# A decoder layer on one core: the self softmax moves to ScalarE, the next batch's queries move behind the attention products, the cross mask goes to GpSimd

## The reference

```
x = x + self_attention(layernorm(x))       # 16 heads of 128; q, k rotated and RMS-normed
    scores = einsum(q, k) * scale; masked causally (-1e30)
    probs  = softmax(concat([scores, sink]))[..., :t]
    y      = probs @ v, then two projections
x = x + cross_attention(layernorm(x), ctx)  # 16 heads of 32
    scores = einsum(q, k) / sqrt(32); masked causally; attn = softmax(scores); out = attn @ v @ Wout.T
x = x + moe(layernorm(x))                   # rmsnorm, router, top 4 of 32 experts, shared expert
```

## Time and profile before

| what | value |
|---|---|
| median of 3 runs | 1218.83 us (1205.28 to 1225.98) |
| the profiled execution | 1214.66 us, span of its instructions 1212.9 us |
| busy over the span | PE 95%, DVE 67%, ACT 49%, POOL 28% |
| one pass of the loop, from PE's L518 to the next | 41.40 us |
| PE's granted clock, mean over the span | 0.979 |

### The profile page before, as it was taken

One profiled execution on the slowest core, in us unless ns is written; L12 is line 12 of the kernel. 1 busy time (PEld: TensorE's weight loads), 2 busy tenths in 40 slices (PEclk: granted clock), 3 DMA queues, 4 the chain that ended last, 5 costly groups with the idle time before them and its releaser, 6 DMA issues. The chain is left out here.

```text
span 1212.9 us, 20949 instructions
## 1 busy us (share of the span) xinstructions
PE 1153.7 (95%) x7761; PEld 910.5 (75%) x7762; DVE 811.2 (67%) x1392; ACT 595.5 (49%) x1404; POOL 336.4 (28%) x279
## 2 busy tenths in 40 slices
PE   6989999999999999999999988899979999999994
PEld 3446777677777767776777666788769999999993
DVE  1144777897888789878977876642256666666661
ACT  1134544654564456445644644321236666666661
POOL 0011013112211212221122112222215666566633
PEclk9998999999999999999999989999989999999997
DMA  7820000000000000000000005032279999999964
GB/s 261 245 96 1 3 3 16 14 9 9 14 15 3 15 14 9 9 16 14 9 9 16 14 10 200 8 122 65 85 250 261 288 285 275 285 291 286 277 143 53
DMA packets 62587, 121.10 MB, mean 100 GB/s; under 512 B 10118, under 2 KB 13750, under 8 KB 62378
## 3 DMA queue, kind: packets, MB, share of 16 engines
q1 hardware_dynamic: 44810, 82.46, 20.3%
q0 software_dynamic: 17728, 37.97, 14.5%
HBM read 93.55 MB, written 28.13 MB: 100 GB/s over the span
## 5 line engine op out<-in xcount | busy, mean ns | idle before, releaser
L1462 POOL TENSOR_TENSOR rall<-qkv_var,phalf 100x17 f32<-100x17 f32 x16 | 49.2, 3073 | 420.5 <-DVE qkv_var L1147 420.5
L379 PE MATMUL QS<-xh,wh 128*128 128x256 f32 x512 | 148.1, 289 | 0.0
L380 PE MATMUL QS<-xl,wh 128*128 128x256 f32 x512 | 145.5, 284 | 0.0
L381 PE MATMUL QS<-xh,wl 128*128 128x256 f32 x512 | 145.4, 284 | 0.0
L1539 POOL DMA_INDIRECT out_rows<-work,idx x64 | 103.0, 1610 | 122.1 <-ACT work L1027 85.1
L379 PE MATMUL W<-wch,oth 128*100 128x512 f32 x256 | 105.1, 411 | 0.0
L380 PE MATMUL W<-wcl,oth 128*100 128x512 f32 x256 | 100.6, 393 | 0.0
L381 PE MATMUL W<-wch,otl 128*100 128x512 f32 x256 | 100.4, 392 | 0.0
L380 PEld LDWEIGHTS QS<-xl,wh 128*128 128x128 f32 x512 | 99.0, 193 | 1.2
L379 PEld LDWEIGHTS QS<-xh,wh 128*128 128x128 f32 x512 | 98.8, 193 | 1.2
L381 PEld LDWEIGHTS QS<-xh,wl 128*128 128x128 f32 x512 | 98.8, 193 | 0.0
(11 more groups left out here) (214 smaller groups left out, 2870.9 us busy)
## 6 DMA issues: line engine op xcount, KB each, us to landing
raw<-in_w SPq DMA_DIRECT2D x24, 1024.0 KB, 8.3
raw<-in_w SPq DMA_DIRECT2D x24, 512.0 KB, 10.2
work<-in_w SPq DMA_DIRECT2D x8, 1024.0 KB, 8.1
work<-in_w SPq DMA_DIRECT2D x8, 512.0 KB, 9.5
hx_rows<-h3x SPq DMA_DIRECT2D x16, 212.5 KB
h_columns<-h3s SPq DMA_DIRECT2D x16, 200.0 KB, 1.9
h3T<-h_columns SPq DMA_DIRECT2D x4, 800.0 KB, 9.8
out_rows<-ytiles POOLq DMA_DIRECT2D x16, 200.0 KB, 2.5
```

The costliest lines, as they stand in the source:

```text
L379: mm(dst, ah, bh, start=start, stop=False)
L380: mm(dst, ah, bl, start=False, stop=False)
L381: return mm(dst, al, bh, start=False, stop=stop)
L1462: return nc.gpsimd.tensor_tensor(out=dst, in0=src, in1=phalf[:, 0:src.shape[1]], op=ALU.pow)
```

## The change

1. Self softmax. DVE takes the maximum of the raw scores straight from each PSUM bank (four reductions), and two 16-wide steps make of it the negative shift per head, with the sink. ACT then takes 16 exponentials, one for each head, from PSUM into SBUF, with the norm as `scale`, the shift as `bias` and the sum over the row as a second output. DVE's scaling, subtraction and sum of the whole go; its last product is cut into four quarters, each with its own signal.
2. ACT's order. The copies of the cross keys, cross values and the next columns stand between the groups of exponentials; the copy of the cross queries behind them; the copy of the cross scores behind the four copies of transposed probabilities.
3. PE's order. The next batch's columns stand in the middle of the cross queries, then keys and values, compressed queries, and the cross scores; the next batch's queries stand behind the attention products. The cross scores wait for all exponentials, since these read the same banks.
4. The cross mask. The four mask products L462 go; GpSimd masks the cross scores in SBUF (`affine_select`, 100 x 1600) after ACT's copy, and DVE's `cross_shifted` waits for it and now stands behind the four L1290.

```
 # tensor, cross_queries(b, more, follow)
                 for i in range(4):
+                    if i == 2 and follow:
+                        ln1_columns(b + 1)
                     for k in range(KC):
                         last = mm(wb[1][:, T * i:T * (i + 1)], w_q[...], h2T[...], ...)
 # tensor, cross_products
-                pe.wait_ge(s.s_scaled, 4 * scored)
+                pe.wait_ge(s.p_exp, scored)
-                for j in range(4):
-                    mm(qb[j][0:T, 0:QW], identb[:, :], mask4[:, :], start=True, stop=False)
 # tensor, step
+                if do.Q:
+                    if do.X:
+                        pe.wait_ge(s.ck, b)
+                    keys_values(b + 1)
+                    if do.X:
+                        pe.wait_ge(s.qp, b)
+                    compress(b + 1)
                 if do.X:
                     cross_products(b, b + 1, do.C)
-                if do.Q:
-                    compress(b + 1)
-                    pe.wait_ge(s.s_scaled, 4 * b + 4)
-                    if do.X:
-                        pe.wait_ge(s.sx, b)
-                    queries(b + 1)
                 if do.A:
-                    pe.wait_ge(s.p_norm, b + 1)
                     for i in range(4):
+                        if i == 1 and do.Q:
+                            pe.wait_ge(s.hqT, b + 2)
                         ...
+                        pe.wait_ge(s.p_norm, 4 * b + i + 1)
 ...
+                if do.Q:
+                    pe.wait_ge(s.p_exp, b + 1)
+                    if do.X:
+                        pe.wait_ge(s.sx, 2 * b - 1)
+                    queries(b + 1)
 # scalar
+            def exponentials(i):
+                for h in range(QH * i, QH * (i + 1)):
+                    last = fn(Pm[0:T, T * h:T * (h + 1)], qb[i][0:T, T * (h % QH):T * (h % QH + 1)], ACT.Exp,
+                              bias=mx[:, h:h + 1], scale=rall[:, h:h + 1], accum_out=den[:, h:h + 1])
+                return last
 # vector, step
-                        tt(Pm[0:T, QW * i:QW * (i + 1)]..., qb[i][0:T, 0:QW]..., per_head(rall[...], QH), ALU.mult)
-                    red(mx[:, :], P3, AX.X, ALU.max).then_inc(s.s_max, 1)
-                    tt(mx[:, :], mx[:, :], sink[:, :], ALU.max).then_inc(s.s_max, 1)
+                        red(mx[:, QH * i:QH * (i + 1)], qb[i][0:T, 0:QW]..., AX.X, ALU.max)
+                    nc.vector.scalar_tensor_tensor(out=mx[:, :], in0=mx[:, :], scalar=-1.0, in1=rall[:, 0:NH], ...)
+                    nc.vector.scalar_tensor_tensor(out=mx[:, :], in0=sink[:, :], scalar=-1.0, in1=mx[:, :], ...)
-                    tt(P3, P3, per_head(mx[:, :], NH), ALU.subtract).then_inc(s.s_shift, 1)
-                    red(den[:, :], P3, AX.X, ALU.add).then_inc(s.p_sum, 1)
-                    tt(P3, P3, per_head(rinv[:, :], NH), ALU.mult).then_inc(s.p_norm, 1)
-                if do.X:
-                    cross_shifted(b)
+                    for i in range(4):
+                        tt(P3[:, QH * i:QH * (i + 1), :], ..., ALU.mult).then_inc(s.p_norm, 1)
                 ... rotate_keys, four differences otl (L1290)
+                if do.X:
+                    cross_shifted(b)
 # gpsimd
+            def cross_masked(b):
+                wait_alone(pool, s.sx, 2 * b - 1)
+                nc.gpsimd.affine_select(out=PX..., in_=PX..., pattern=[[0, NX], [-1, T]],
+                                        compare_op=ALU.is_ge, fill=NEG, base=0, channel_multiplier=1).then_inc(s.sx, 1)
```

More of the change, by code:

```diff
@@ L406, in ln1_columns, with keys_values @@
                 to_columns(wb[0], h1).then_inc(s.h1T_ps, 1)
+            def keys_values(c):
+                pe.wait_ge(s.h1T, c + 1)
+                for k in range(KC):
+                    last = mm(wb[2][0:T, 0:2 * D], h1T[:, T * k:T * (k + 1)], w_kv[:, 256 * k:256 * (k + 1)],
+                              start=k == 0, stop=k == KC - 1)
+                last.then_inc(s.kv_ps, 1)
             def compress(c):
@@ L414, in compress @@
                 last.then_inc(s.hq_ps, 1)
[L415 to L418, removed]
             def queries(c):
@@ L432, in project, with cross_queries @@
                 return last
-            def cross_queries(b, more):
+            def cross_queries(b, more, follow):
                 pe.wait_ge(s.ln2_h, b)
@@ L468, in cross_products @@
                         last = mm(qb[j][0:T, T * i:T * (i + 1)], qpT[r, T * i:T * (i + 1)],
-                                  ckT[r, T * i:T * (i + 1)], start=False, stop=i == 3)
+                                  ckT[r, T * i:T * (i + 1)], start=i == 0, stop=True,
+                                  skip_group_check=True)
                 last.then_inc(s.sx_ps, 1)
@@ L623, in _ @@
             ln1_columns(0)
+            keys_values(0)
             compress(0)
@@ L812, in compressed @@
                 copy(kvs[:, :], wb[2][0:T, 0:2 * D]).then_inc(s.kv, 1)
+                act.wait_ge(s.hq_ps, c + 1)
+                act.wait_ge(s.q_ps, 4 * c)
+                copy(hqT[:, :], wb[1][:, 0:T]).then_inc(s.hqT, 1)
             def queries_out(c):
@@ L860, in step @@
                     copy(h2T[:, :], wb[0][:, 0:QW]).then_inc(s.h2T, 1)
+                if do.A:
+                    act.wait_ge(s.s_shift, 2 * b + 2)
+                    act.wait_ge(s.pT_ps, 4 * b)
+                    act.wait_ge(s.p_den, 2 * b)
+                    exponentials(0)
+                if do.X:
                     act.wait_ge(s.ck_ps, b)
@@ L863, in step @@
                     copy(ckT[:, :], wb[2][:, 0:QW]).then_inc(s.ck, 1)
+                if do.A:
+                    exponentials(1)
+                if do.X:
                     act.wait_ge(s.cv_ps, b)
@@ L866, in step @@
                     copy(cv[:, :], wb[3][0:T, :]).then_inc(s.cv, 1)
+                if do.A:
+                    exponentials(2)
+                if do.Q:
+                    ln1_columns(b + 1)
+                if do.A:
+                    exponentials(3).then_inc(s.p_exp, 1)
+                    act.wait_ge(s.s_sink, b + 1)
+                    fn(esink[:, :], sdiff[:, :], ACT.Exp).then_inc(s.e_sink, 1)
+                if do.X:
                     act.wait_ge(s.qp_ps, b)
@@ L869, in step @@
                 if do.Q:
-                    ln1_columns(b + 1)
+                    compressed(b + 1)
+                    key_square(b + 1)
                 if do.A:
[L872 to L875, removed]
-                    fn(esink[:, :], sdiff[:, :], ACT.Exp).then_inc(s.e_sink, 1)
+                    act.wait_ge(s.s_ps, 4 * b + 4)
+                    for i in range(4):
+                        act.wait_ge(s.pT_ps, 4 * b + i + 1)
+                        copy(T16[0:T, QW * i:QW * (i + 1)], wb[i][0:T, 0:QW]).then_inc(s.pT, 1)
                 if do.X:
@@ L1281, in step @@
                     dve.wait_ge(s.p_den, 2 * b + 2)
-                    tt(P3, P3, per_head(rinv[:, :], NH), ALU.mult).then_inc(s.p_norm, 1)
-                if do.X:
-                    cross_shifted(b)
+                    for i in range(4):
+                        tt(P3[:, QH * i:QH * (i + 1), :], P3[:, QH * i:QH * (i + 1), :],
+                           per_head(rinv[:, QH * i:QH * (i + 1)], QH), ALU.mult).then_inc(s.p_norm, 1)
                 if do.Q:
@@ L1479, in step @@
                     ln1(b + 1)
+                if do.X:
+                    cross_masked(b)
+                if do.Q:
                     qk(b + 1)
```

60 lines of the change are left out of this document (28 added, 32 removed).

## The result

The changed kernel takes 1248.13 us in the median, the kernel before 1224.19 us in the same comparison: ratio 1.0235, 95% interval 1.0187 to 1.0283. One of its six runs was disturbed (4443 us) and is left out of the ratio; the other five lie between 1239.47 and 1254.35. So the changed kernel is slower; whether by more than 2% is not settled, since 2% lies inside the interval. The forecast was 1242.5 us, by a mechanism in three pieces.

What follows compares the result with a forecast made beforehand. PE was taken to bound the loop; stalls of 2.4 us less 0.77 saved cost 1.6 a pass, 14 x 1.6 + 1 = 23.5 us: 1238 for the profiled execution, 1242.5 on the median, range 1218 to 1268.

Steps and rivals of the forecast that it cites:

- a mechanism in three pieces: PE stalls each pass: 0.85 us at the columns, 1.15 before keys and values, 0.4 before compress.
- Bound and cost of a stall: In the loop PE has no slack: waits are paid in full; its work falls 0.77 to 40.6 us a pass.
- First stall: At the next batch's columns, mid cross queries, PE waits 0.85 us for DVE, itself held by POOL's late power.
- The exponentials: ACT's 16 exponentials cost 0.41 us each (bounds 0.23 and 0.50), so h1T is done late, at 463.35.
- the sum of stalls: PE's waits in one loop pass: 0.85 + 1.15 + 0.4 = 2.4 us, before the 0.77 saved.
- The mask: GpSimd's mask before DVE's cross shift takes 2.5 us, hidden; up to 3.5 before PE stalls.
- The room behind: Later in the pass nothing stalls: 0.45 us of room before the queries, 0.6 before PE's transposes at 485.8.
- The ends: Outside the 14 loop passes: batch 0 about +2 us, batch 15 some 1.5 sooner, tail +1.5 less 0.8; together +1.
- (a): Rival, chance 0.17: operands hidden, 0.23 to 0.27 us an exponential; only the columns' stall stays, 1221 us.
- (b): Rival, chance 0.15: GpSimd's mask becomes the bound beyond 3.5 us; at 5 us, 1.5 more a pass, 1265 us.
- (c): Rival, chance 0.10: new stalls lower PE's clock for 3.3 us a pass, half of that lost, 1266 us.
- (d): Rival, chance 0.05: faster, 1205 to 1207 us, with columns ready 0.85 us sooner and exponentials under 0.32 us.

Runs made afterwards that it cites:

- x2: Changed kernel with the next batch's columns back behind the cross queries instead of in their middle; 1267.92 us, run once.
- x3: Changed kernel with the 16 exponentials without both per-partition operands (fixed scale 0.01, no bias; probabilities not the reference's); 1227.33 us, run once.
- x5: Changed kernel with one per-partition operand (the bias) and a fixed scale of 0.01 in the exponentials; probabilities not the reference's; 1246.63 us, run once.
- x1: Kernel before with only the mask change: mask products gone, GpSimd masks between ACT's copy and DVE's shift; 1241.30 us, ratio 1.0119.
- x9: Kernel before without mask products; GpSimd writes zeros after ACT's cross exponential, cross values' product behind the cross queries; ratio 1.0018.
- x12: x9 with ACT's copy cv and the sink's exponential moved behind the copies hqT and kvs; ratio to the kernel before 1.0033.
- x6: Changed kernel with GpSimd's mask done three times over, one after the other; 1325.10 us, run once.
- x10: Kernel before without mask products; GpSimd masks ahead of DVE's maximum, cross values' product behind the cross queries; ratio 1.0197.
- x4: Changed kernel with the edits of x2 and x3 together; probabilities not the reference's; 1217.27 us, run once.
- x8: Changed kernel with the next batch's queries ahead of the transposes again, the cross scores' copy ahead of the transposes' copies; 1337.78 us, run once.

## Why the prediction was right, and where not

**Bound and cost of a stall: right.** PE bounded before and bounds after, at a clock of 1.00, and its waits are paid in full: 0.85 + 1.12 + 0.35 less 0.77 is 1.55 of the 1.66 us; the remaining 0.1 is the hand-over between compress and the cross products. PE's busy time, forecast as 40.6, reads 41.14, since around each wait a modelled end runs on.

**First stall: right,** 0.85 us, with POOL's power behind its four list transfers. But passes 2 and 3 of x2 show that it is no term by itself: with the columns back, PE waits for h1T by as much longer. What sets the pass is ACT's chain.

**The exponentials: right.** Forecast 0.41 us by adding the operands of the earlier trace rows to a Square of the earlier trace rows, measured 0.41; x3 and x5 show both terms, 0.23 and 2 x 0.09. Set back by the 11.86 us, ACT's h1T starts at 462.78, forecast 462.85, and the sum of stalls is 2.32 against 2.4.

**The mask: right that it is hidden, its price too high.** Taken 2.5 us, measured 1.64; the nearest row, DVE's pass of 1.81, was the better estimate than the middle of the bounds. Because it was hidden, nothing followed.

**The room behind: right.** L496 was forecast 485.8, and is 485.83 in those positions. The queries did not wait.

**The ends: the mis-sized term.** Forecast +1 beside 14 passes of 1.6. Batch 15 is 1.7 us shorter (forecast 1.5), but the tail pass is 2.3 longer and what follows it 2.2, where 0.7 was forecast. The rows, which answer:

```profile
735.23 1.67 PE L472 MATMUL QS<-ckT,qpT 32*100 32x100 f32 x32 [3.73 <-ACT qpT L806]
...
779.31 0.45 PE L379 MATMUL QS<-h3h,w_suh 128*128 128x400 f32 x1 [3.32 <-DVE w_sul L1366]
```

In batch 15 the wait has moved from the transposes to the cross products, where qpT now stands behind 16 exponentials; it is in one piece, and the products behind it run at the slower level (1.67 us against 0.96). In the tail PE waits 3.32 us for DVE's w_sul, 1.54 before. DVE had waited on its way there:

```profile
773.38 1.82 DVE L1206 TENSOR_REDUCE mxx<-work 100x16 f32<-100x1600 f32 x1 [1.52 <-POOL work L1510]
```

POOL's mask stands there behind four list transfers and takes 2.11 us, and unlike in the loop nothing lies between DVE and it. This wait was priced rightly (1.5). What the prediction put at nothing is the clock behind the waits. The 8.28 us of PE's work that follow the wait for w_sul have a mean granted clock of 0.79, and took 6.71 us at 1.00 before; the stretch behind them gives back 1.0. A little later, behind the last cross output, stands a wait of 3.00 us for DVE's h3x, which the kernel before has too (3.01), and only in the changed one is the work behind it slow:

```profile
809.99:816.33 6.34, 6.34 (x29) 6.32 (x30) 3.30 (x4) 2.72 (x4) 0.00 (x0) 0.73 0.10 35
```

Before, this stretch took 4.81 us at 1.00. Whether the change brings this is open: x1, x3, x5, x9 and x12 show 0.96 over the 47 us behind the last cross output too, as the changed kernel does, and only one execution of the kernel before was traced.

Start and loop went the other way: batch 0 and 14 passes were forecast at 24.4 us and brought 21.8. Batch 0 is 1.8 us longer, as forecast (38.44 against 36.63, between the starts of the transposes L541, L546 after). But it starts 0.9 us sooner, for which no run gives a cause, and pass 1 is 0.3 us shorter and not 1.6 longer (42.83 against 43.13): in the kernel before it ran in part at the slower level (L541 took 2.87 us, 1.72 in the later passes), and that is a matter of the one execution. Two errors of 2.6 and 3.6 us, of opposite sign; that the profiled time came so near the forecast is luck in this part.

**The whole.** 1238 us was forecast for the profiled execution, 1239.5 came. (The sum is rounded up twice: 14 x 1.6 + 1 is 23.4, and 1218.83 + 23.5 is 1242.3. Neither matters.) The median was forecast 1.9% above the one before, and is 2.35% [1.87, 2.83] above: the profiled execution is the fastest of the five. What the others have more is in no trace here; the part behind the loop, which varies by 20 us between the traces, is one place where it can lie.

**The rivals.** (a) fell: the operands are not hidden. Its condition, an exponential under about 0.32 us, is borne out by pass 3 of x3 and x5 (41.89 and 41.86 us); its pass of 0.08 us more than before was 0.31 more there, since the wait at the columns is 1.23 us in that pass. With the late hand-over the passes of x3 took 42.28 us. (b) fell, its mechanism is real (x6). (c) did not come in passes 2 to 14, and x2 shows how near it was; its 3.3 us at the slower level come from no row, and in x2 the clock was low over 6 us. (d) did not come: it asked for columns 0.85 us sooner and for cheap exponentials. Pass 2 of x3 has both, and there the 0.77 us are won, as (d) says; with the list transfers in POOL's queue and their order changed it was not tried. In the order of the kernel before, the same 0.77 us were not to be had (x1, x9 to x12), since the mask products covered the copy qpT there.

## What to carry to other kernels

Where an engine is busy without a gap, each piece of its work also covers a hand-over to another engine; before counting the removal of 0.77 us as a gain, read which copies end within the next 0.77 us. When work goes from one long instruction to sixteen short ones, price the chain by starts (here 0.41 us each, of which 0.18 are operands), and then ask what stands in that engine's queue behind it. And put GpSimd's work where DVE reads PSUM or has one input: beside an add with two inputs in SBUF the mask of 1.64 us held the add until its own end (x1, x10). Last, when an experiment undoes one of several stalls, look at the pass and not at the stall: in x2 one of 0.85 us went and the pass stayed as long.

## What the hardware showed that was not expected

- A 16-wide add on DVE took 1.39 and 1.50 us instead of 0.17 beside a GpSimd mask (x1, x10).
- About 2.3 us of waiting a pass in three pieces left the clock at 1.00; 2.0 us in one piece was followed by 0.62 and 0.76 over the next 6 us in pass 5 of x2, but not in its pass 3, and after 1.65 us in one piece in x4 the pass kept 1.00. In the changed kernel PE waited 1.8 us in one piece for h1T in passes 1 and 2; the keys and values behind it took 3.63 us in pass 1 and 1.94 in pass 2.
- GpSimd's mask of 100 x 1600 took 1.64 us in the loop, less than DVE's pass over the same columns (1.81).
- PE's hand-over of the ckT product came 2 us later in x2 to x8 than in the two kernels compared, from pass 4 on, with PE's rows in the same places. Its cause is open.
